# Output projection of a causal attention stage: from float32 products to products of high and low parts, with the parts made by GpSimd

## The reference

```
q, k, v = (xn @ w_q), (xn @ w_k), (xn @ w_v)      # 256 -> 1024, 16 heads of 64
dot = einsum('bqhd,bkhd->bhqk', q / 8, k / 8)     # causal mask, softmax over k
out = einsum('bhqk,bkhd->bqhd', att, v)           # the context, 1024 wide
return out @ w_u + b_u                            # the output projection, 1024 -> 256
```

## Time and profile before

| | |
|---|---|
| median of 3 runs | 2040.0 us (2035.83 to 2042.59) |
| profiled execution: its time | 2041.42 us |
| its span in the trace | 2039.7 us |
| mean granted PE clock | 0.953 of full |
| busy, whole span | PE 91%, DVE 65%, ACT 32%, POOL 9% |
| stage of the change | about 373 us of the span |

### The profile page before, as it was taken

How to read it: one execution, slowest core, us unless ns; L and a number is a source line. 1 busy time by engine, 2 the same in 40 slices (tenths; PEclk the granted TensorE clock), 3 DMA queues, 4 the chain that set the end, 5 groups by cost and what they waited for, 6 DMA issues and landing times. The chain is left out here.

```text
span 2039.7 us, 43767 instructions
## 1 busy us (share of the span) xinstructions
PE 1856.5 (91%) x16819; PEld 1549.4 (76%) x16819; DVE 1326.4 (65%) x3598; ACT 649.3 (32%) x1504; POOL 175.9 (9%) x125
## 2 busy tenths in 40 slices
PE   6999999699759999999999868878899999999998
PEld 5877787577548888888888735557688888888887
DVE  4555555377668888888788546656666665656564
ACT  3444344244421211221121024435433332333332
POOL 0000000111000000000000054631000000000000
PEclk9999999799879999999999969989899999999999
DMA  4000000221060000000000040001111111111101
GB/s 156 1 1 0 0 0 1 63 68 41 7 129 2 7 7 3 7 7 8 2 7 1 2 117 1 0 1 37 25 24 26 21 25 22 24 22 24 22 0 42
DMA packets 139320, 48.61 MB, mean 24 GB/s; under 512 B 108179, under 2 KB 138419, under 8 KB 139187
## 3 DMA queue, kind: packets, MB, share of 16 engines
q1 hardware_dynamic: 139186, 46.66, 10.2%
HBM read 42.43 MB, written 4.19 MB: 23 GB/s over the span
## 5 line engine op out<-in xcount | busy, mean ns | idle before, releaser
L2840 DVE TENSOR_TENSOR m_act_up<-m_silu,m_up 128x512 f32<-128x512 f32 x136 | 93.4, 687 | 168.4 <-PE m_up L587 125.3
L2759 ACT ACTIVATE m_silu<-m_gate 128x512 f32<-128x512 f32 x136 | 81.5, 599 | 380.0 <-PE m_gate L587 380.0
L2824 DVE SCALAR_TENSOR_TENSOR g_x<-m_y,m_combine,g_x 128x256 f32<-128x256 f32 x272 | 118.8, 479 | 53.0 <-PE m_y L587 51.4
L233 ACT ACTIVATE a_prob<-a_score,a_neg_max 128x128 f32<-128x128 f32 x256 | 90.6, 367 | 170.2 <-DVE a_neg_max L223 170.2
L2404 PE MATMUL f_out<-f_ko,f_gel 128*128 128x256 f32 x512 | 128.4, 404 | 0.9 <-DVE f_gel L2580 0.7
L2447 ACT ACTIVATE f_gel<-f_act 128x512 f32<-128x512 f32 x128 | 76.6, 599 | 132.3 <-PE f_act L587 90.9
L2404 PEld LDWEIGHTS f_out<-f_ko,f_gel 128*128 128x128 f32 x512 | 100.3, 203 | 15.9 <-issue 1.5
L2404 PE MATMUL f_turn<-f_ko,f_gel 128*128 128x256 f32 x512 | 111.8, 379 | 0.0
L587 PE MATMUL f_act<-f_hT_pair_high,f_kiT_high 128*128 128x256 f32 x384 | 108.2, 282 | 0.0
L2404 PEld LDWEIGHTS f_turn<-f_ko,f_gel 128*128 128x128 f32 x512 | 97.3, 190 | 13.2
L587 PE MATMUL f_act<-f_hT_pair_low,f_kiT_high 128*128 128x256 f32 x384 | 107.3, 279 | 0.0
(11 more groups left out here) (381 smaller groups left out, 5022.7 us busy)
## 6 DMA issues: line engine op xcount, KB each, us to landing
f_gel<-in_L_ffn_key_in SPq DMA_DIRECT2D x16, 256.0 KB, 4.8
f_ko<-in_L_ffn_key_out SPq DMA_DIRECT2D x2, 2048.0 KB, 18.4
g_shared<-in_ctx SPq DMA_DIRECT2D x8, 256.0 KB, 2.7
fp_wq_nat<-in_L_ffn_w_q SPq DMA_DIRECT2D x8, 256.0 KB, 3.1
h_kept<-fp_hT SPq DMA_DIRECT2D x8, 256.0 KB, 2.9
g_shared<-h_kept SPq DMA_DIRECT2D x8, 256.0 KB, 3.4
g_ctx_next<-in_ctx SPq DMA_DIRECT2D x8, 256.0 KB, 2.7
g_ctx_all<-in_ctx SPq DMA_DIRECT2D x1, 2048.0 KB, 10.4
```

What stands on the lines that cost most here:

```text
L233: last = act.activation(self.prob[:, u % 4, j, :], self.score_bank[u % 2][:, j // 2, (j % 2) * P:(j % 2 + 1) * P], ACT.Exp, bias=self.neg_ ...
L2759: act.activation(silu[:, m, :], gate_bank[m][:, :], ACT.Silu).then_inc(silu_ready[m].sem, 1)
L2824: last = dve.scalar_tensor_tensor(x[:, tile, :], y_bank[n][:, t * D:(t + 1) * D], weight, x[:, tile, :], ALU.mult, ALU.add)
L2840: dve.tensor_tensor(act_up[:, m, :], silu[:, m, :], up_bank[m][:, :], ALU.mult) \
```

## The change

The output projection becomes a `split_product` too: three float32r matmuls for each float32 one, 48 in a pair instead of 16. The parts of the context and of w_u are made by POOL. For each chunk POOL multiplies `attnT(c)` by a one (an operand broadcast from one column) into the high part and subtracts it from `attnT(c)` into the low part; PE waits for `parts_ready` at four places of the projection. For w_u the same two instructions run once, on 2048 elements per partition, ahead of POOL's loop, and PE waits for `wu_ready` ahead of its own loop instead of `out_loaded`. To find room, w_u is loaded over w_q's natural copy, and the context takes w_k's place: so the load of w_u waits on SP until the low part of w_q is made (`low_ready` 1), and b_u and the rest of x are issued behind it.

```diff
+        self.part_links = Chain(s.sem("part_links"), self.chunks)
+        self.parts_ready = s.counting("parts_ready", self.chunks)
+        self.one = s.sb("one", [P, 1])
+        self.one_set = s.sem("one_set")
...
+    def pool_parts(self, pool, i, c, high, low):
+        if c == 0:
+            self.part_links.begin(i)
+        pool.wait_ge(self.out_ready.sem, self.out_ready.at(i, c + 1))
+        if c == 0:
+            pool.wait_ge(self.projected, i)
+        self.part_links.link(pool, pool.tensor_tensor(high, self.attnT(c), self.one[:, 0:1].broadcast_to([P, 4 * P]), ALU.mult))
+        pool.tensor_tensor(low, self.attnT(c), high, ALU.subtract).then_inc(self.parts_ready.sem, 1)
+
     def pe_project(self, pe, i, terms):
         pe.wait_ge(self.out_ready.sem, self.out_ready.at(i, self.chunks))
         for b in range(2):
             pairs = terms(b)
+            half = len(pairs) // 2
             for n, (a, w) in enumerate(pairs):
-                last = pe.matmul(self.out_bank[:, b * D:(b + 1) * D], a, w, start=(n == 0), stop=(n == len(pairs) - 1))
+                if n % half == 0:
+                    pe.wait_ge(self.parts_ready.sem, self.parts_ready.at(i, 2 * b + n // half + 1))
+                last = split_product(pe, self.out_bank[:, b * D:(b + 1) * D], a, w, n == 0, n == len(pairs) - 1)
         last.then_inc(self.projected, 1)
...
-        wu = s.sb("wu", [P, MT, D])
+        wu_nat = w_nat[:, 0, :, :].rearrange("p k (t d) -> p (k t) d", d=D)
+        wu = [s.sb(f"wu_{part}", [P, MT, D], F32R) for part in ("high", "low")]
...
-        attnT = s.sb("attnT", [P, 2, MT, P])
+        attnT = w_nat[:, 1, :, :].rearrange("p k (t q) -> p k t q", q=P)
+        attn_parts = [s.sb(f"attnT_{part}", [P, 2, MT, P], F32R) for part in ("high", "low")]
...
-            sp.dma_start(wu[:, :, :], w_u.rearrange("(k p) n -> p k n", p=P)).then_inc(out_loaded, 16)
+            sp.wait_ge(low_ready, 1)
+            sp.dma_start(wu_nat[:, :, :], w_u.rearrange("(k p) n -> p k n", p=P)).then_inc(out_loaded, 16)
             sp.dma_start(bu[:, :], on_all_partitions(b_u)).then_inc(out_loaded, 16)
...
             pool.wait_ge(out_loaded, 32)
+            pool.memset(att.one[:, :], 1.0).then_inc(att.one_set, 1)
+            pool.wait_ge(att.one_set, 1)
+            pool.tensor_tensor(wu[0][:, :, :], wu_nat[:, :, :],
+                               att.one[:, 0:1].unsqueeze(2).broadcast_to([P, MT, D]), ALU.mult).then_inc(wu_ready, 1)
+            pool.wait_ge(wu_ready, 1)
+            pool.tensor_tensor(wu[1][:, :, :], wu_nat[:, :, :], wu[0][:, :, :], ALU.subtract).then_inc(wu_ready, 1)
             for i, _ in pairs_by_two(pool):
                 att.add_bias(pool, i, x, bu, ln)
+                att.pool_parts(pool, i, 0, *[chunk_of(part, 0) for part in attn_parts])
                 ln.root(pool, i + 2)
+                for c in range(1, 4):
+                    att.pool_parts(pool, i, c, *[chunk_of(part, c) for part in attn_parts])
...
             att.pe_first(pe, qT, kT)
-            pe.wait_ge(out_loaded, 32)
+            pe.wait_ge(wu_ready, 2)
...
-                att.pe_project(pe, i, lambda b: [(attnT[:, b, t, :], wu[:, t, :]) for t in range(MT)])
+                att.pe_project(pe, i, lambda b: [([part[:, b, t, :] for part in attn_parts], [part[:, t, :] for part in wu])
+                                                 for t in range(MT)])
```

More of the change, by code:

```diff
@@ L378, in stage_causal_attention, with chunk_of @@
         v = [s.sb(f"v{n}", [P, 2, HW]) for n in range(2)]
-        attnT = s.sb("attnT", [P, 2, MT, P])
+        attnT = w_nat[:, 1, :, :].rearrange("p k (t q) -> p k t q", q=P)
+        attn_parts = [s.sb(f"attnT_{part}", [P, 2, MT, P], F32R) for part in ("high", "low")]
         ln = LayerNorm(s, x)
         ring = Ring(s, SLOTS)
-        att = CausalAttention(s, ident, (ident_bf, mask_bf),
-                              lambda c: attnT[:, c // 2, 4 * (c % 2):4 * (c % 2) + 4, :].rearrange("p t q -> p (t q)"),
+        def chunk_of(part, c):
+            return part[:, c // 2, 4 * (c % 2):4 * (c % 2) + 4, :].rearrange("p t q -> p (t q)")
+        att = CausalAttention(s, ident, (ident_bf, mask_bf), lambda c: chunk_of(attnT, c),
                               vector_copies=(0, 2, 4, 6))
@@ L388, in stage_causal_attention @@
         low_ready = s.sem("low_ready")
+        wu_ready = s.sem("wu_ready")
         xn_high = s.counting("xn_high", 1)
```

## The result

The changed kernel took 2026.07 us (median of 4 runs, 2024.73 to 2028.44), the kernel before on the same chip 2040.6 (4 runs): ratio 0.994 [0.9924, 0.9956]. Timed once more (after_again) the ratio was 0.9956 [0.9941, 0.9972]. So it is faster, by 9 to 12 us by these ratios, where 7 were forecast. The profiled execution of the changed kernel took 2028.44 us, that of the kernel before 2041.42.

A forecast was written before the change was run, and what follows sets the result against it. PE was taken to set the pace in the attention stage, except in the last pair (DVE and ACT). Terms -9.4 + 0.3 + 0.7 + 1.3 = -7.1 us, from 2040.0, gave 2033; range 2028 to 2041, the forecast's own 2030 to 2036.

The forecast's parts named there:

- PE per pair: Output projection in the attention stage: 48 float32r matmuls take 5.84 us instead of 7.01, -9.4 us over eight pairs.
- POOL per pair: Attention pairs: POOL's splitting adds 10.3 us a pair, 2.6 a chunk, hidden in its idle time, so costs nothing.
- Port waits in pairs: Attention pairs: DVE and POOL take turns at shared SBUF ports, +0.3 us over steady pairs, +0.7 in the last.
- The start: Before the attention loop: POOL's high part of w_u holds DVE's third low part, delaying PE by 1.3 us (0.7 to 2.5).
- The rival that POOL takes the ports first: At the start, b_u lands early and POOL holds DVE's second low part, 4.8 us on PE; total 2037.6; chance 15%.
- The five other stages are the same program, so they only shift.: Stages after attention: they begin after a barrier and only start earlier, with no change of their own.

The follow-up runs named there:

- after_parts_late: The changed kernel, but POOL waits for the third low part of the weights before making w_u's parts: 2022.48 us, ratio 0.9922; run again 2026.44 us, 0.9948.
- after_first_stage: The changed kernel with the five later stages left out, x stored after the attention stage: 380.67 us (5 runs).
- before_first_stage: The kernel before with the five later stages left out, x stored after the attention stage: 385.59 us (5 runs).
- after_118_spread: The changed kernel with 118 more PE instructions, 64, 28 and 26 in three places where PE waits anyway: 2037.97 us, ratio 1.0002.
- before_138_spread: The kernel before with 138 more PE instructions, 64, 28 and 46 in three places where PE waits anyway: 2028.22 us, ratio 0.9961.
- before_again: The kernel before, unchanged, run again: 2037.65 us, ratio 0.9999.
- before_shift: The kernel before with one DVE memset behind DVE's last attention-stage instruction, to start later stages about 1.3 us later: 2037.99 us, ratio 0.9999.
- before_pe_138_more: The kernel before with 138 more PE instructions (276 already fulfilled waits) at the very start: 2037.39 us, ratio 0.9997.
- after_pe_118_more: The changed kernel with 118 more PE instructions (236 already fulfilled waits) at the very start: 2038.72 us, ratio 1.0001.

## Why the prediction was right, and where it wasn't

The direction came out as forecast, and 2033 is 4 to 7 us above what was measured; the first median, 2026.07, lies 2 us below the range. But the agreement is in large part luck: a cost that was too small and a gain that no step had. Of the 13.0 us between the two profiled executions the forecast's own stage gave 2.2, and product keys, which the forecast had at nothing, 11.7.

- **PE per pair, -9.4.** Right: 1.16 us a pair for 1.17. The spacing of 0.12 us taken from slots 2 and 3 is that of the 48 matmuls.
- **POOL per pair, nothing.** Right. Its parts cost 2.3 us a chunk unhindered (2.5 on the mean, with waits for DVE), less than the 2.6 taken, and no wait of PE for them is seen.
- **Port waits in pairs, +0.3 and +0.7.** About right. DVE's L246 and L156 and POOL's L313 are longer by 0.3 to 1.0 us in turns, as forecast from the gated stage. With the start mended, the stage's gain was 7.6 and 7.0 us (373.4 less 365.8 and 366.4), where the terms without the start give -9.4 + 0.3 + 0.7 = -8.4. So the pairs give back 1.7 to 2.3 of 8 x 1.16 = 9.3 us, instead of 1.0; that all of it is waits for the ports is argued, not shown.
- **The start, +1.3 (0.7 to 2.5): the step that failed.** The mechanism was right, a low part of DVE held by POOL for a whole instruction. The moment at which POOL comes agreed too, 24.9 by the forecast and 25.06, but by luck: the forecast had POOL kept out by DVE's second low part until then, while in the trace b_u had only just landed (24.88) and that low part still ran to 25.73. The term was mis-sized: it had the high part hold the third low part from 28.74 to 30.0. But the high part took 4.14 us, not 5.1 (3.60 unhindered, in after_parts_late; the rest was its wait for DVE's second low part), and was through at 29.20; and DVE came 0.84 us later, at 29.58, since its parts ahead were a little late too (14.80 and 23.45 for 14.52 and 22.62). Between the two POOL's *low* part slipped in, at 29.28, and held DVE for 4.1 us. DVE's lateness is not needed for that: in after_first_stage the third low part came at 27.97 for 27.90 in before_first_stage, and POOL's low part, at 27.68, was ahead of it as well. The working had a high part that ends too late, and never asked what follows if it ends early: at that turning point the price jumps from nothing to a whole instruction. Nor was the clock in it: PE's 4.23 us of waiting were followed by the stretch at 0.62. Together +5.8. The Trainium skill, "GPSIMD Engine Reference", section 3.1, gives 4.5 us for POOL's instruction of this size: the subtraction of two full operands measured 4.55 and 4.56, the multiplication by a repeated column 3.60, so for the latter the measurement decides.
- **The rival that POOL takes the ports first** put 4.8 us on the second low part. It happened, to the third.
- **"The five other stages are the same program, so they only shift."** This is the other step that failed. They are the same instructions at another place. Before, one of the nine loads of instructions in an iteration of the product-keys loop came late for a gather, in all seven passes of the first trace and in six of seven of the second. Over the seven passes, against 0.95 us for an unhindered one, that is 10.8 - 6.7 = 4.1 us directly. The rest of the 8.5 to 11.7 goes with the clock, for the most part: in the stage it stood at half for 72.6 us before and 57.9 after, and in the second pair of traces for 62.8 and 57.4. If PE sets the pace there, that is an estimated 7.3 and 2.7 us, so the second pair leaves 1.7 open. That the late instructions bring the lower clock about is argued from this, and from the fact that the kernels with an unhindered gather have 585.7 to 589.2 us and those with a hindered one 591.5 to 600.0. Against it stands after_118_spread, hindered in four passes of seven and at half clock for only 54.5 us. No run holds the clock fixed.

**What the change is worth by itself.** In its own stage 2 to 4 us: 2.2 by the two pairs of traces, 4.4 by the runs of the stage alone. In the whole kernel no gain can be told from none: with the loop at the place of before it is 1.0002 [0.9985, 1.0019], and with the loop at the place of after, before_138_spread has 0.9961 [0.9946, 0.9977] where the changed kernel has 0.9956 [0.9941, 0.9972]. In the traces of the changed kernel part of what its stage gains is given back by the chunked stage, 166.6 and 167.0 us against 163.9 and 164.8. That isn't tied to the change: the changed kernel with 118 more instructions at the start has 164.0 there, after_parts_late 164.9. The chunked stage's busy time by stretch, before_again and then after_again, differs in the clock:

```profile
373.30:537.20 163.90, 136.82 (x1936) 103.39 (x1936) 105.90 (x166) 64.99 (x115) 17.79 (x23) 0.91 0.21 54
```

```profile
371.10:538.10 167.00, 140.75 (x1936) 105.97 (x1936) 105.90 (x166) 64.98 (x115) 17.80 (x23) 0.88 0.20 53
```

The same 1936 matmuls take 3.9 us longer. before_138_spread has a clock of 0.93 there and 161.6 us. Why one kernel gets 0.93 and another 0.88 stays open. The one run meant to move the moment of the start left it as it was (before_shift: 164.0), and no run varied it finely.

## What to carry to other kernels

Where an engine takes turns at a shared port, follow it through *each* of its instructions, and ask what it costs if one of them starts just ahead of the one that matters; one wait (`low_ready`, 3) was worth 5 us of the stage here. Adding or removing instructions of one stage moves the code of every later loop: look at the loads of instructions and at `issue` waits in the stages that the diff doesn't touch, and time the kernel before with as many idle instructions before you credit a change with a gain of half a per cent. Put such instructions where the engine waits anyway, or their own time hides what they show.

## What was not expected of the hardware

- A loop of PE with 846 matmuls and as many weight loads a pass was reloaded in each iteration, nine packets of 16 KB in 70 us, at some places in the program, and hardly at all at another: 51 and 2 packets in 400 us. With the loop 138 instructions on, the loads vanish; with 64 or 256 they stay. The rule behind it stays open.
- Such loads cost nothing in most places: with 64 more instructions there are 105 of them and no gather takes over 0.97 us. Inside a run of short matmuls (64 in 0.89 us) PE ran dry for up to 1.2 us.
- POOL multiplies by one repeated column in 1.04 us where the subtraction of two full operands takes 1.27 (512 elements), and in 3.60 against 4.55 (2048).
- DVE's L156, 128x256 with its scalars, was held by POOL too: 1.70 us for a pair of instructions that take 0.73.
- Waits on PE that are fulfilled already are not free: the 40 more that before_pe_138_more has over after_pe_118_more (276 and 236) took 2.1 us (19.61 less 17.53), 0.05 each.
